# Linear attention and gated MLP on one core: a reordered ramp with four V buffers, output pieces added in place, a spill in four

## The reference, cut to what matters

```
xn = layernorm(x)
q, k, v = xn @ wq.T, xn @ wk.T, xn @ wv.T          # q, k rotated (rope)
per chunk of 64: o = (q k^T * decay) v + (q * q_decay) kv
                 kv = block_decay * kv + (k * k_decay)^T v
s = o @ wo.T
g = silu( fp8mm( silu(fp8mm(xn, gate)) * fp8mm(xn, up), down ) )
out = x + s * g
```

## Time and profile before

| | us |
|---|---|
| median of 3 runs | 949.07 |
| profiled execution | 949.77 |
| its span | 948.0 |
| TensorE busy (matmul) | 906.7 (96%) |
| VectorE (DVE) busy | 628.3 (66%) |
| ScalarE (ACT) busy | 421.3 (44%) |
| GpSimd (POOL) busy | 363.0 (38%) |

### The profile page before, as it was taken

How to read it: one execution, slowest core, us unless ns; L and a number is a source line. 1 busy time by engine, 2 the same in 40 slices (tenths; PEclk the granted TensorE clock), 3 DMA queues, 4 the chain that set the end, 5 groups by cost and what they waited for, 6 DMA issues and landing times.

```text
span 948.0 us, 12465 instructions
## 1 busy us (share of the span) xinstructions
PE 906.7 (96%) x4128; PEld 743.5 (78%) x4128; DVE 628.3 (66%) x915; ACT 421.3 (44%) x709; POOL 363.0 (38%) x267
## 2 busy tenths in 40 slices
PE   5799999999899999999999999999999999989996
PEld 4588888878688887888888888888888878867776
DVE  7676672676753256666787766786756677957686
ACT  3443533443532456445355445455454454533531
POOL 0011211221212475535535545455455455343541
PEclk9899999999999999999999999999999999989999
DMA  7683303468651524422333504333503333428272
GB/s 241 209 275 116 129 12 134 156 236 286 244 220 46 200 88 153 148 66 112 133 124 126 205 23 155 133 112 133 198 34 133 117 146 135 154 80 260 72 222 78
DMA packets 50971, 138.55 MB, mean 146 GB/s; under 512 B 4208, under 2 KB 25840, under 8 KB 45424
## 3 DMA queue, kind: packets, MB, share of 16 engines
q1 hardware_dynamic: 50928, 138.00, 41.9%
HBM read 96.04 MB, written 41.94 MB: 146 GB/s over the span
## 4 chain that ended last, share of the span: by engine, by line
PE 38%; issue 30%; POOL 19%; DVE 6%; DMA 4%; ACT 2%; SPq 1%; POOLq 0%; DVEq 0%; ACTq 0%
PE bank L1175 37%; POOL d_r L1133 11%; POOL rot L1142 8%; DMA v_decayed<-vd_split 1%; DMA out_t<-fin 1%; DMA stage<-in_x_nat 1%; DMA tail_sb<-mlp_gate 1%; ACT gout L507 1%; DVE xn L761 1%; DMA v_split<-gout 0%; DMA vs<-v_split 0%; DVE vd_split L832 0%; DVE q_r L952 0%; DVE d_sb L959 0%; PE bank L1209 0%
## 5 line engine op out<-in xcount | busy, mean ns | idle before, releaser
L1175 PE MATMUL bank<-xn,aw 128*128 128x512 f32 x960 | 228.7, 389 | 0.0
L1142 POOL TENSOR_TENSOR rot<-rot 128x512 f32<-128x512 f32 x80 | 127.8, 1598 | 237.1 <-DVE rot L946 237.1
L1175 PEld LDWEIGHTS bank<-xn,aw 128*128 128x128 f32 x960 | 179.3, 188 | 36.6
L1175 PE MATMUL bank<-xn,gu_w 128*128 128x512 f32 x768 | 183.4, 394 | 7.6 <-DVE xn L761 5.5
L1133 POOL TENSOR_TENSOR d_r<-d_sb,d_r 128x512 fp32r<-128x512 f32 x128 | 166.8, 1331 | 61.1 <-ACT d_r L646 60.9
L1175 PE MATMUL bank<-o_r,ow 128*128 128x512 f32 (+1 forms) x816 | 186.6, 379 | 0.0
L1175 PEld LDWEIGHTS bank<-xn,gu_w 128*128 128x128 f32 x768 | 145.9, 190 | 39.3 <-DVE xn L761 5.7
L1175 PEld LDWEIGHTS bank<-o_r,ow 128*128 128x128 f32 x816 | 145.7, 188 | 27.6
L646 ACT CAST d_r<-d_sb 128x512 fp32r<-128x512 f32 x128 | 78.9, 621 | 110.3 <-DVE d_sb L1004 68.8
L945 DVE TENSOR_TENSOR rot<-bank,rope 128x512 f32<-128x512 f32 x80 | 55.2, 690 | 97.1 <-ACT rot L626 96.8
L625 ACT COPY rot<-bank 64x512 f32<-64x512 f32 x80 | 46.7, 584 | 146.0 <-PE bank L1175 145.5
(11 more groups left out here) (73 smaller groups left out, 949.8 us busy)
## 6 DMA issues: line engine op xcount, KB each, us to landing
xn<-xn_split SPq DMA_DIRECT2D x15, 2048.0 KB, 7.9
v_decayed<-vd_split SPq DMA_DIRECT2D x32, 512.0 KB, 3.3
vd_r<-v_decayed SPq DMA_DIRECT2D x16, 1024.0 KB, 6.8
xn_split<-xn SPq DMA_DIRECT2D x4, 2048.0 KB, 9.1
v_r<-v_split SPq DMA_DIRECT2D x16, 512.0 KB, 5.8
wst<-in_mlp_w SPq DMA_DIRECT2D x10, 768.0 KB, 5.2
stage<-in_attn_w SPq DMA_DIRECT2D x4, 1280.0 KB, 5.8
stage<-in_x_nat SPq DMA_DIRECT2D x16, 256.0 KB, 4.5
```

Source lines behind the costliest of these rows:

```text
L1142: pool.tensor_tensor(rot1[:, r % RRING, :], rot1[:, r % RRING, :], rot2[:, r % RRING, :], ALU.add).then_inc(qk_sum, 1)
L1175: last = pe.matmul(dst, a, b, start=start and x == 0, stop=stop and x == len(pairs) - 1)
```

## The change

The pieces of the first two slabs come in the order gate 0, up 0, gate 1, up 1, down 0, down 1. The first eight V tiles have four buffers (two in `gout`, two in slabs 4 and 5, 6 and 7 of `f_all`) with a semaphore each. TensorE makes the high-high products of the first V tiles between the transposes, and V tiles 4 to 7 between the second batch's transposes and its first gate-up unit; DVE's, ACT's and SP's lists follow. Tiles 12 to 15 are transposed at slabs 4 to 7, one later. The spill of the last batch is four DMAs at slabs 8 to 11. `finish` adds in place in one of four pairs of buffers (`stage` grew by the two tiles of the old `fin`), the next batch's pieces are loaded once their pair is stored, and piece 0 is stored ahead of `load_xn`. The diff, cut to its core (left out: the semaphores' declarations and counts that follow, and the one-slab shift on each engine):

```diff
-PIECES = [(m, c * KT * P, (c + 1) * KT * P) for m in range(SLABS) for c in range(PARTS)] + [(m, 0, WHOLE) for m in range(SLABS, MT)]
+PIECES = ([(m, c * KT * P, (c + 1) * KT * P) for c0, c1 in ((0, 2), (2, PARTS)) for m in range(SLABS) for c in range(c0, c1)]
+          + [(m, 0, WHOLE) for m in range(SLABS, MT)])
...
-VT_AT = {(1, m): TT + m - 1 for m in range(1, 1 + TT)} | {(2, m): 2 * TT + m for m in range(TT)} | {(3, m): 3 * TT + m for m in range(TT)}
+VT_AT = {(2, m): 2 * TT + m for m in range(TT)} | {(3, m): 3 * TT + m for m in range(TT)}
 NV = NB * TT
 VSLOT = 2
+VFIRST = 4
+SPILL = 4
+LND = 4
...
-        fin = sb("fin", [P, 2, S])
-        assert nc.sbuf_base >= early_end
-        stage = sb("stage", [P, XRING, KT * P])
+        stage_all = sb("stage", [P, 2 * KT, KT * P])
+        stage = stage_all[:, 2 * KT - XRING:, :]
+        assert nc.sbuf_base >= early_end + XRING * KT * P * 4
...
-        v_first = gout[:].rearrange("p (r a) (g e) -> p r a g e", r=VSLOT, g=NG)
+        v_first = [t.rearrange("p (r a) (g e) -> p r a g e", r=2, g=NG) for t in (gout[:], f_all[:, KT:2 * KT, :])]
...
-        fin_in = stage[:].rearrange("p (r t) s -> p r t s", t=2)
+        fin = stage_all[:].rearrange("p (u t) s -> p u t s", t=2)
...
-            return bank[4 + v] if v < TT else bank[7]
+            return bank[4 + v] if v < TT else bank[v - TT] if v < 2 * TT else bank[7]
 
         def v_slot(v):
 
-            return v_first[:, v % VSLOT] if v < 2 * TT else vs[:, v % VSLOT]
+            return v_first[v % VFIRST // 2][:, v % 2] if v < 2 * TT else vs[:, v % VSLOT]
+
+        def v_ring(v):
+
+            return (v % VFIRST, v // VFIRST) if v < 2 * TT else (VFIRST + v % VSLOT, (v - 2 * TT) // VSLOT)
...
+            def spill_last(i):
+                a, k = i // 2, i % 2 * 2
+                sp.wait_ge(ln_lo, NB * TT)
+                sp.dma_start(xn_dram[ORDER[NB - 1], :, a, k:k + 2, :], xn0[:, a, k:k + 2, :].bitcast(F32)).then_inc(xn_out, 16)
...
             store_v(0)
             load_w(2)
-            for v in range(1, TT):
+            for v in range(1, TT + 1):
                 store_v(v)
             load_w(3)
+            for v in range(TT + 1, 2 * TT):
+                store_v(v)
+            load_w(4)
             spill_xn(0)
-            load_w(4)
             for i in range(2 * TT, 3 * TT):
                 load_x(i)
+            load_w(5)
             spill_xn(1)
-            for m in range(5, MT):
-                if m - 5 < TT:
-                    store_v(TT + m - 5)
+            for m in range(6, MT):
                 load_w(m)
...
                     if s == 2 and m in (3, 5, 7, 9):
                         fetch_v((m + 1) // 2)
-                    if (s, m) == (2, 8):
-                        spill_xn(3)
+                    if s == 2 and m >= MT - SPILL:
+                        spill_last(m - (MT - SPILL))
+                    if (s, m) == (2, MT - SPILL):
                         sp.wait_ge(ln_t, NB * TT)
                         sp.dma_start(stage[:, 0:PT, :], attn_w[0]).then_inc(aw_in, 16)
...
             def load_fin(b, u):
-                sp.dma_start(fin_in[:, u % FINR, 0, :], x_t[u, :, bass.ts(b, S)]).then_inc(fin_ld[u % FINR], 16)
-                sp.dma_start(fin_in[:, u % FINR, 1, :], g_dram[u, :, bass.ts(b, S)]).then_inc(fin_ld[u % FINR], 16)
+                if b >= 1:
+                    sp.wait_ge(stored[u], 16 * b)
+                sp.dma_start(fin[:, u, 0, :], x_t[u, :, bass.ts(b, S)]).then_inc(fin_ld[u], 16)
+                sp.dma_start(fin[:, u, 1, :], g_dram[u, :, bass.ts(b, S)]).then_inc(fin_ld[u], 16)
+
+            def store_fin(b, u):
+                sp.wait_ge(fin_d, b * KT + u + 1)
+                sp.dma_start(out[u, :, bass.ts(b, S)], fin[:, u, 0, :]).then_inc(stored[u], 16)
...
-                    if final and b < NB - 1:
-                        if b == 0:
-                            sp.wait_ge(ow_lo, g * HG + HG)
-                        for u in range(FINR):
+                    if final and b == 0:
+                        sp.wait_ge(ow_lo, g * HG + HG)
+                        for u in range(KT):
...
+                    if final and b < NB - 1:
+                        store_fin(b, 0)
                     if not (final and b >= NB - 2):
                         load_xn(n + 1, (b + 2) % NB)
                     if final and b < NB - 1:
-                        for u in range(KT):
-                            sp.wait_ge(fin_d, b * KT + u + 1)
-                            sp.dma_start(out[u, :, bass.ts(b, S)], fin[:, u % 2, :]).then_inc(stored[u % 2], 16)
-                            if u + FINR < KT:
-                                load_fin(b, u + FINR)
-                            if b == NB - 2:
+                        if b == NB - 2:
+                            load_tail(0)
+                        for u in range(1, KT):
+                            store_fin(b, u)
+                            if b < NB - 2:
+                                load_fin(b + 1, u - 1)
+                            else:
                                 load_tail(u)
+                        if b < NB - 2:
+                            load_fin(b + 1, KT - 1)
...
             w_floor(1)
-            for v in range(TT):
+            for v in range(TT - 1):
                 v_round(v)
-            act.wait_ge(const_in, 16)
             for i in range(TT, 2 * TT):
                 norm(i)
-            w_floor(2)
+            act.wait_ge(const_in, 16)
             silu_gate(0, 0)
+            v_round(TT - 1)
             for i in range(TT, 2 * TT):
                 norm_hi(i)
+            w_floor(2)
+            w_floor(3)
             fuse_hi(0)
-            for q in range(PARTS, 2 * PARTS):
-                w_floor(q)
+            v_round(TT)
+            w_floor(4)
+            v_round(TT + 1)
+            w_floor(5)
+            v_round(TT + 2)
+            w_floor(6)
+            v_round(TT + 3)
             silu_gate(1, 0)
-            w_floor(2 * PARTS)
...
                 norm_lo(i)
             w_exponent(0)
             w_exponent(1)
+            tile_stats(TT)
+            tile_stats(TT + 1)
+            w_round(0)
+            tile_stats(TT + 2)
+            tile_stats(TT + 3)
+            mean_var(2)
             v_rest(0)
-            w_round(0)
+            inv_std(2)
             w_round(1)
-            v_rest(1)
-            for i in range(TT, 2 * TT):
-                tile_stats(i)
-            mean_var(2)
-            v_rest(2)
+            for v in range(1, TT):
+                v_rest(v)
             w_exponent(2)
-            inv_std(2)
-            v_rest(3)
-            w_round(2)
+            w_exponent(3)
             dve.wait_ge(const_in, 16)
             fuse(0, 0)
-            for q in range(PARTS, 2 * PARTS):
-                w_exponent(q)
             for i in range(TT, 2 * TT):
                 norm_lo(i)
-            w_round(PARTS)
-            w_round(PARTS + 1)
+            w_round(2)
+            w_round(3)
+            w_exponent(4)
+            v_rest(TT)
+            w_round(4)
+            w_exponent(5)
+            v_rest(TT + 1)
+            w_round(5)
+            v_rest(TT + 2)
+            w_exponent(6)
+            v_rest(TT + 3)
             fuse(1, 0)
-            w_round(PARTS + 2)
-            w_exponent(2 * PARTS)
...
                 dve.wait_ge(acc_d, n * KT + KT + u + 1)
-                loads = len(range(u % FINR, KT, FINR))
-                dve.wait_ge(fin_ld[u % FINR], b * (32 * loads) + (u // FINR + 1) * 32)
-                dve.tensor_tensor(fin_in[:, u % FINR, 1, :], acc[:, b, u, :], fin_in[:, u % FINR, 1, :],
-                                  ALU.mult).then_inc(fin_p, 1)
+                dve.wait_ge(fin_ld[u], b * 32 + 32)
+                dve.tensor_tensor(fin[:, u, 1, :], acc[:, b, u, :], fin[:, u, 1, :], ALU.mult).then_inc(fin_p, 1)
                 dve.wait_ge(fin_p, b * KT + u + 1)
-                if u >= 2:
-                    dve.wait_ge(stored[u % 2], (b * (KT // 2) + u // 2) * 16)
-                else:
-                    if_later(b, lambda: dve.wait_ge(stored[u % 2], b * (KT // 2) * 16))
-                dve.tensor_tensor(fin[:, u % 2, :], fin_in[:, u % FINR, 1, :], fin_in[:, u % FINR, 0, :],
-                                  ALU.add).then_inc(fin_d, 1)
+                dve.tensor_tensor(fin[:, u, 0, :], fin[:, u, 1, :], fin[:, u, 0, :], ALU.add).then_inc(fin_d, 1)
...
+            def v_part(v, parts):
+
+                s, j = divmod(v, TT)
+                for x in parts:
+                    a, c = SPLIT[x]
+                    last = products(v_bank(v)[:], [(xn_of(s)[:, a, k, bass.ts(j, P)], wv[:, c, k, :]) for k in range(KT)],
+                                    start=x == 0, stop=x == len(SPLIT) - 1)
+                return last
+
+            def v_first_high(v):
+
+                pe.wait_ge(ln_hi, v + 1)
+                if v == 0:
+                    pe.wait_ge(wv_hi, KT)
```

(64 more changed lines are left out.)

41 lines of the change are left out of this document (18 added, 23 removed).

## The result

The changed kernel takes 925.75 us (median of 4 runs, 924.73 to 926.07), beside 949.81 for the kernel before in the same comparison (4 runs): ratio 0.9746, 95% interval 0.9729 to 0.9763. The profiled execution took 924.73, its span 922.9, against 949.77 and 948.0 before.

What follows compares the result with a forecast made beforehand. TensorE, busy 906.7 of 948.0 us, was taken as the bound. Gains 9.8 + 1.5 + 2.8 + 10.5 = 24.6 us gave 925.2 from the profile and 924.5 from the timed runs, stated as 925, range 920 to 931.5.

Steps and rivals of the forecast that it cites:

- Ramp, 9.8: First batches up to m = 5: V tiles 4 to 7 moved into TensorE's idle hole gain 9.8 us, between 5 and 12.
- The first high products: Start of the ramp: 16 high products and two remaining transposes run to 16.1 us, 32 low ones to 23.4.
- the hole before V tile 4: Ramp, after the second batch's transposes end at 28.9: TensorE idles about 1.8 us, in place of 5.47.
- The 3.3 us for the lower clock: Old ramp: 48 products after the 5.47 us wait took 14.15 instead of 10.9 us, about 3.3 lost.
- The price of 0.36 us for four transposes: Full-clock price used in the ramp's walk: four transposes take about 0.36 us on TensorE.
- Transposes, 1.5: Last batch's transposes one slab later: the wait on bank 7, shared with V tile 11, goes; gain 1.5 us, bounds 0 and 1.6.
- Spill, 2.8: Last batch's spill in four: decayed V's store lands 4.6 us sooner, ACT's wait falls to about 5; gain 2.8 us.
- Last group, 10.5: Last group, adds in place: DVE's 4.07 us wait goes, three steps of 37.5 us; gain 10.5 us, bounds 8.5 and 12.9.
- The waits that SP got for freed pairs: Last group: SP's loads of the next batch's pieces wait for stores; V loads some 3 us late, about 9 to spare.
- Tail, 0: End of the kernel: unchanged, its last load still follows the store of piece 3.
- starving slabs: Rival, ramp: slabs arrive late if the queue runs under 140 GB/s; at 130, 954 us; chance 0.02.
- The rival that the clock falls in the ramp: Rival, new ramp: the clock falls all the same around the transposes, price 3.3 us, 928.3 us; chance 0.12.

## Why the prediction was right

The forecast was 925, measured 925.75; the sum of gains was 24.6 for the profile, measured 25.0 (949.77 - 924.73).

- **Ramp, 9.8: measured 9.56**, but two steps inside were off and cancelled, and how much the ramp gains depends on the pair of executions, 7.6 to 9.9 us; that the total came so close is in part luck. The first high products were put at full clock, V of the first batch ending at 23.4; in fact the first four took 2.04 us, the transposes and the next four were slow too, and it ended at 24.9. For the same reason the hole before V tile 4, put at 1.8 us, was 0.41: TensorE came to it later, while DVE and ACT kept to their times (low halves from 30.1, forecast 30.0; v_rest(7) at 45.1, forecast done by 44.9). The rate at which the slabs follow, 9.07 us, was right. The walk had each list's times, yet it priced the V tiles as filler for one 5.47 us wait. Taken away, they cost 8.2 to 10.5 us, since behind that wait stands a second, for the weights' rounding, and the lower clock. That four buffers were needed was said without a price: 4.3 us, of which the trace gives 3.26 to the wait. The 3.3 us for the lower clock were a little high and held for one execution: the 48 products took 14.15, 13.02 and 13.24 us in the three traces of the old ramp, and 48 at full clock take 11.19, so it cost 3.0, 1.8 and 2.1. The price of 0.36 us for four transposes is not to be read from the earlier trace rows; the changed kernel's trace bears it out (15.32 to 15.68).
- **Transposes, 1.5: 1.63**, and 1.6 by undoing it.
- **Spill, 2.8: 3.47**, and 3.3 by undoing it. ACT's wait was put at about 5 us and was 4.75.
- **Last group, 10.5: 9.86**, and 9.5 alone. The steps were to be 37.5 and are 37.50, 37.96, 37.74: two of them keep 0.46 and 0.24 us more than forecast, 113.20 us together for 112.5. The cause, a store behind a 2 MB load, is shown by moving the store alone. The waits that SP got for freed pairs had no reader, as forecast: with the store late the time stayed.
- **Tail, 0: 0.4 of DVE's wait**, 2.7 instead of 3.1.

Of the rivals, starving slabs would have needed a queue under 140 GB/s; it ran at 376 to 414. The rival that the clock falls in the ramp fell as well: of the short stretch of transposes alone and 0.41 us of waiting nothing is seen in the clock. The Trainium skill's rule that spoke for it ("TensorE: Matmul & The Clock Gate", Part 4: PE-mode transpose, transposes do not count as busy work) did not bring a lower clock here, but it is not refuted either. Against it: with two V buffers 16 transposes and 3.67 us of waiting, 5.57 us without a product, left the clock at 1.00 (32 to 36 us). For it: in the two other traces of the old ramp the clock fell to 0.50 at 34.0 and 34.4 us, only 2.0 and 2.5 us after the end of 16 transposes, while behind plain products it fell 2.7 us into the idle time at the earliest. In the trace of the kernel before it fell at 36.4, 4.4 us after the transposes. So with the same 5.47 us wait the moment of the fall differs by more than 2 us between executions, and these traces can't separate the rule from that.

## What to carry to other kernels

Before putting work into a hole of the bounding engine, list what stands behind the hole: the moved work also covers the waits that would come next, and its worth is the sum of them with the lower clock, not the one wait that the table shows. A wait for a buffer can be a wait for a queue: look at what was issued just ahead of the DMA that frees it, and move either. Here all DMAs have one issuer, and the large ones (2 MB and 1.3 MB) delayed the small stores behind them; so cut such a one up, or set it where the small ones have slack, and issue a load with free space ahead of a store that still waits.

## What the runs showed of the hardware that was not expected

- At the start of the trace TensorE ran at about half rate for some 4 us, with a granted clock of 1.00 in the profile's stretches. In every kernel that has products between the first transposes, the first four took 2.02 to 2.05 us (0.51 each, at full clock 0.227) and the second four 1.17 to 1.99. With 16 transposes in one go it is these that are slow, 3.52 to 3.80 us against 1.91 later, and the four products behind them took 1.18 to 1.54 where the trace has them apart. Why the clock record does not show it is open.
- Behind idle stretches of 0.4, 1.5 and 2.2 us, and once of 3.67, the clock stayed at 2.4 GHz; after 3.94, 4.2, 5.47 and 6.51 us a stretch partly at 1.2 GHz followed, which cost 1.8 to 3.0 us each. When it falls is not fixed: in three executions with the same 5.47 us wait it fell 2.0, 2.5 and 4.4 us after TensorE's last work.
- The DMA queue moved up to 414 GB/s over 10 us with loads and stores mixed.
